# A two-layer graph network on one NeuronCore: the first part with an on-chip sort and a turned edge MLP in place of a dealt scatter

## The chip, the cores and the metric

The kernel runs on one NeuronCore of a Trainium2 chip. The metric is the device time of one execution in microseconds (us), the median over several executions; lower is better.

## The reference, cut to what matters

There are 3125 nodes with 128 features and 100000 edges, sorted by `dst`, with 64 features each. Two graph layers follow each other, each with a residual sum and a layer norm. The change lies in what comes before the first layer's softmax: the MLP on the edges (three small heads), and the records that both layers read.

```python
h = node_features @ node_fc_W + node_fc_b
he = edge_features @ edge_fc_W + edge_fc_b
t = relu(einsum('ed,mdf->emf', he, rel_att_W1) + rel_att_b1)      # m = 3, f = 128
g = sigmoid(einsum('emf,mf->em', t, rel_att_W2) + rel_att_b2)     # 3 numbers for each edge
a = sum(h[src] * h[dst]);  alpha = seg_softmax(a, dst);  beta = seg_softmax(g, dst)
h_att = segment_sum(alpha * (h[src] @ node_att_W), dst)
h_rel = segment_sum(beta * (h[src] @ rel_att_W), dst)
# layer 1: softmax over the edges of one src
e = tanh(q[src] + k[dst]);  alpha = exp(e @ Wphi) / segment_sum(..., src)
out = segment_sum(alpha * (vy[dst] + e @ We), src)
```

## The kernel before, in words

The program is a row of blocks, and all engines end one before the next begins.

**The first part** (lines 300 to 790) makes two tables of records in DRAM: `rec0`, the edges in `dst` order with src, dst and the three exponentials of the sigmoids (10 words), and `rec1`, the pairs (src, dst) grouped by blocks of 125 source nodes, which layer 1 reads. An edge table in SBUF has 125 lanes by 800 edges. VectorE (DVE) counts how many edges of each lane fall into each of 25 blocks (L622), for both keys. A plan is made of the counts: 220 steps for each layer, each a group of 512 edges with a block of nodes. Then DVE works out each edge's place in `rec1` (`place_step`, L661 to L667, four operations on 125x800 for each of 25 blocks), and GpSimd scatters the pairs, 125 at a time, by indirect DMA (`scatter`, L414, 580 of them); DVE stages them (L691, L696). The last 220 columns of the edge table (`late`) are scattered in the next block, one for each of its steps (L859).

The MLP runs in the same part, 200 chunks of 500 edges. SyncE (SP) loads a chunk; TensorE (PE) transposes it (L508), ScalarE (ACT) copies the result to SBUF (L586), PE multiplies four times with the folded weights (L517, 125 edges by 384 hidden values each, with the bias as an extra row), and DVE takes each of the 12 pieces of 125x128 through relu, product with W2 and sum in one operation (`weigh`, L703). Scatter staging, the places in `dst` order and `weigh` alternate in DVE's queue by a fixed order (`deal_turn`); `dealt` semaphores hold DVE until a slot's scatter has landed. Then come the sigmoid, the exponentials and a split of the weights into three bf16 parts (L758 to L762), and four DMAs store `rec0` (L368).

**The second block** (L840 to L1070) is layer 0, 220 steps of 512 edges. In each step SP loads a record group and a block of h, GpSimd issues one scatter of `late` (L859) and four gathers of 128 rows of h (L863) into a ring of five, PE transposes them (L879, L885), makes scores (L896) and sums (L909, L912, L918), ACT and DVE do the softmax and the accumulation (L1005, L1019). **The fourth block** is layer 1 with the same steps over `rec1` (L1361 gathers kv rows); the third and the last block are per-node work.

Of the kernel before, what the change touches and what calls it, by code (L numbers as in the profile page):

```python
# [24 lines left out]
M = 3  # L25
# [16 lines left out]
LATE = STEPS  # L42
EARLY = (EL - LATE) // 4
DEAL = 6
SLOTS1 = 3
# [7 lines left out]
PIECES = 4  # L53
assert EL % PIECES == 0
assert EARLY * 4 + LATE == EL and EARLY == DEAL * (NB - 1) + 1 and DEAL == 2 * SLOTS1
# [18 lines left out]
def build(nc, i, out):  # L74
    with ExitStack() as ctx:
# [15 lines left out]
        rec1 = dram("rec1", [PADDED, W2], I32)  # L91
        plan_d = [dram(f"plan_d{l}", [STEPS, 2], I32) for l in range(2)]
        rec0_v = rec0.rearrange("(g p j) w -> g p (j w)", p=128, j=GT)
        rec1_v = rec1.rearrange("(g p j) w -> g p (j w)", p=128, j=GT)
# [28 lines left out]

        late = sb("late", [LANES, LATE, 1 + W2], I32)

# [57 lines left out]
        with ExitStack() as c1:  # L183
# [7 lines left out]
            scratch = rel_st[:, :, :].rearrange("p b n -> p (b n)")  # L191

            def part(n, dt=F32):
                return scratch[0:LANES, n * EL:(n + 1) * EL].bitcast(dt)

            src_i, dst_i = part(0, I32), part(1, I32)
            blk, sel, run, place, zero = (part(n) for n in range(2, 7))
            place_i = [part(n, I32) for n in (7, 8)]
            sel2, run2 = part(9), part(10)
            pair = sb1("pair", [LANES, EL, 2], I32)  # L200
            cnt = sb1("cnt", [LANES, 2, NB])
            tot = sb1("tot", [128, 2, NB])
            incl = sb1("incl", [128, 2, NB])
            off = sb1("off", [128, 2, NB])
            first = sb1("first", [LANES, 2, NB])
# [4 lines left out]
            cmp_t = sb1("cmp_t", [GH, 2, 2, NB - 1])  # L210
# [9 lines left out]
            pad1 = sb1("pad1", [PAD_LANES, GT, W2], I32)  # L220
# [5 lines left out]
            weT = sb1("weT", [DE, DE + 1])  # L226
            w1 = sb1("w1", [DE, M, D])
            w1b = sb1("w1b", [1, M * D])
            w2 = sb1("w2", [LANES, M, D])
            b2 = sb1("b2", [LANES, M])  # L230
            last_row = sb1("last_row", [1, DE + 1])
            wc = sb1("wc", [128, M * D])
            whole = sb1("whole", [LANES, 1])
            flag = sb1("flag", [1, 1], I32)
            iota_e = sb1("iota_e", [LANES, EL])
# [5 lines left out]
            ea = sb1("ea", [LANES, U, 4 * DE])  # L241
            eaT = sb1("eaT", [128, 2, 4 * LANES])
            hid = sb1("hid", [LANES, 4, M, D])
            glog = sb1("glog", [LANES, U, 4 * M])
            eg = y_sb[:, :, :].rearrange("p b d -> p (b d)")[0:LANES, 0:EL * M]
            rem = att_st[:, :, :].rearrange("p b d -> p (b d)")[0:LANES, 0:EL * M]
            U16 = mybir.dt.uint16
            rec_all = arena[0:LANES, 0:EL * RW].bitcast(I32).rearrange("p (e w) -> p e w", w=RW)
            rec_f = arena[0:LANES, 0:EL * RW].rearrange("p (e w) -> p e w", w=RW)
            rec_b = arena[0:LANES, 0:EL * RW].bitcast(BF16).rearrange("p (e w) -> p e w", w=2 * RW)  # L250
            rec_h = arena[0:LANES, 0:EL * RW].bitcast(U16)
            st_rec0 = sb1("st_rec0", [LANES, U, 4 * RW], I32)
            st_rec1 = sb1("st_rec1", [LANES, U, 4 * W2], I32)
# [3 lines left out]
            edges_in = sem1("edges_in")  # L257
            weights_in = sem1("weights_in")
            counted = sem1("counted")
# [11 lines left out]
            staged = [sem1(f"staged{l}") for l in range(2)]  # L271
            dealt = [[sem1(f"dealt{l}_{k}") for k in range((U, SLOTS1)[l])] for l in range(2)]
# [3 lines left out]
            folded = sem1("folded")  # L276
            x_in = sem1("x_in")
# [11 lines left out]
            tiled = sem1("tiled")  # L289
            g_sb = sem1("g_sb")  # L290
            biased = sem1("biased")
            flag_ps = sem1("flag_ps")
            flagged0 = sem1("flagged0")
            flagged = sem1("flagged")
            in_order = sem1("in_order")
            linear = sem1("linear")
            sig = sem1("sig")
            weighed = sem1("weighed")

            ea_dram = i["edge_attr_64"].rearrange("(p t) c -> p (t c)", p=LANES)  # L300
            WEIGHT_DMAS = 21

            with nc.Block() as block:
                @block.sync
                def _(sp):
# [5 lines left out]
                        (we[:, :], i["L0_gnn_edge_fc_W"]), (weT[:, DE:], col(i["L0_gnn_edge_fc_b"])),  # L311
                        (w1[:, :, :], i["L0_gnn_rel_att_W1"].rearrange("m d f -> d m f")),
                        (w1b[:, :], row(i["L0_gnn_rel_att_b1"].rearrange("m f -> (m f)"))),
                        (w2[:, :, :].rearrange("p m f -> p (m f)"),
                         i["L0_gnn_rel_att_W2"].rearrange("m f -> (m f)").partition_broadcast(LANES)),
                        (b2[:, :], i["L0_gnn_rel_att_b2"].partition_broadcast(LANES)),
# [8 lines left out]
                        (w_e1[:, :], i["L1_gnn_We"]), (phi_b[:, :], i["L1_gnn_Wphi"].partition_broadcast(128)),  # L325
                        (x_sb[:, :, :], i["x"].rearrange("(b p) d -> p b d", p=BN)),
                    ]
                    assert len(loads) == WEIGHT_DMAS
# [3 lines left out]
                    sp.wait_ge(pads, 4)  # L332
                    sp.dma_start(rec0[E:, :].rearrange("(p j) w -> p (j w)", j=GT),
                                 pad0[:, :, :].rearrange("p j w -> p (j w)")).then_inc(pads_out, 16)
                    sp.dma_start(rec1[E:, :].rearrange("(p j) w -> p (j w)", j=GT),
                                 pad1[:, :, :].rearrange("p j w -> p (j w)")).then_inc(pads_out, 16)
# [8 lines left out]
                    for k in range(U):  # L345
                        sp.dma_start(ea[:, k, :], ea_dram[:, k * 4 * DE:(k + 1) * 4 * DE]).then_inc(ea_in[k], 16)

                    sp.wait_ge(plan_ready, 1)
                    for l in range(2):
                        sp.dma_start(plan_d[l].rearrange("(p h) k -> p (h k)", h=2),  # L350
                                     plan_i[0:STEPS // 2, l, :, :].rearrange("p h k -> p (h k)")).then_inc(plan_out, 16)
                    sp.wait_ge(plan_out, 32)
                    for l in range(2):
                        flat_plan = plan_d[l].rearrange("s k -> (s k)")
                        sp.dma_start(plan_row[l][:, :], row(flat_plan)).then_inc(plan_in, 16)
                        sp.dma_start(plan_b[:, l, :, :].rearrange("p s k -> p (s k)"), flat_plan.partition_broadcast(128)).then_inc(plan_in, 16)
                    with sp.Fori(1, CHUNKS // U) as c:
                        for k in range(U):
                            sp.wait_ge(ea_ps, U * c + k + 1 - U)
                            sp.dma_start(ea[:, k, :], ea_dram[:, bass.ds((c * U + k) * 4 * DE, 4 * DE)]).then_inc(ea_in[k], 16)  # L360

                    sp.wait_ge(flagged, 1)
                    ordered = sp.value_load(flag[0:1, 0:1], min_val=0, max_val=1)
                    with sp.If(ordered == 1):
                        for n in range(PIECES):
                            cols = slice(n * EL * RW // PIECES, (n + 1) * EL * RW // PIECES)
                            sp.wait_ge(in_order, n + 1)
# [167 lines left out]
                def _(act):  # L535
# [51 lines left out]
                    for k in range(U):  # L587
                        turned(0, k, k < 2)
# [1123 lines left out]
```

## Time and profile before

| what | us |
|---|---|
| median of 3 runs | 4611.61 (4606.64 to 4620.9) |
| the profiled execution | 4621.28, its span 4619.5 |
| busy PE, DVE, POOL, ACT | 3162.4, 2799.3, 2950.0, 1186.1 |
| mean granted TensorE clock | 0.815 of full |

Engines' busy times overlap, so they don't add up to the span. A time in the rows below is a place in the span; a group's "idle before" is how long its engine stood still ahead of it, with what released it.

### The profile page before, as it was taken

How to read it: one execution, taken by the hardware profiler on the slowest of the kernel's cores; microseconds unless marked ns; L12 is line 12 of the kernel's file. 1: busy time of each engine (PE TensorE's matmuls, PEld its weight loads, DVE VectorE, ACT ScalarE, POOL GpSimd, SP SyncE). 2: the span in 40 equal slices, each digit the busy share in tenths (PEclk: the TensorE clock that was granted, in tenths of full speed). 3: DMA queues.
4: the chain of work that ended last, by engine and by line, in shares of the span. 5: the costliest groups of instructions: out<-in, count | busy, mean ns of one | idle time of the engine just before them, and what ended most of it. 6: DMA issues, size and time to landing. Idle time of an engine off the chain costs nothing. (4 is left out here: it accounts for less than half of the span.)

```text
span 4619.5 us, 75532 instructions
## 1 busy us (share of the span) xinstructions
PE 3162.4 (68%) x16479; PEld 2217.2 (48%) x16479; DVE 2799.3 (61%) x11134; ACT 1186.1 (26%) x3211; POOL 2950.0 (64%) x2590
## 2 busy tenths in 40 slices
PE   5177777776477887878878777855666666666664
PEld 3043444443255555555555555634545554554453
DVE  5977777777455555555555555564555555555554
ACT  2011111111133333333333333412222222222222
POOL 0088888886467777777767777405666666666661
PEclk9599899898688998888889889955777677767776
DMA  2011111111211221211212212102222222222221
GB/s 70 4 29 29 29 28 29 28 28 22 68 42 44 45 45 43 45 43 43 45 41 45 44 44 45 24 23 67 69 71 71 71 71 71 71 70 70 71 70 28
DMA packets 298189, 218.99 MB, mean 47 GB/s; under 512 B 215607, under 2 KB 269234, under 8 KB 298144
## 3 DMA queue, kind: packets, MB, share of 16 engines
q0 software_dynamic: 96000, 146.02, 13.7%
q1 hardware_dynamic: 202144, 72.47, 6.8%
q8 instruction: 15, 0.25, 0.0%
q14 instruction: 30, 0.25, 0.0%
HBM read 203.84 MB, written 13.22 MB: 47 GB/s over the span
## 5 line engine op out<-in xcount | busy, mean ns | idle before, releaser
L1361 POOL DMA_INDIRECT arena<-kv_table,rec_sb x880 | 906.4, 1030 | 479.4 <-issue 238.8
L863 POOL DMA_INDIRECT arena<-h_table,rec x880 | 998.3, 1134 | 270.4 <-issue 262.5
L414 POOL DMA_INDIRECT rec<-st_rec,st_at x580 | 737.4, 1271 | 387.6 <-issue 386.4
L517 PE MATMUL bank<-wc,eaT 128*125 128x384 f32 x1600 | 626.5, 539 | 327.1 <-DVE hid L703 221.9
L909 PE MATMUL bank<-arena 128*128 128x375 f32 x1760 | 617.5, 494 | 0.0
L1407 PE MATMUL bank<-arena,probT 128*125 128x193 f32 x1760 | 513.5, 456 | 118.0 <-DVE probT L1525 61.7
L517 PEld LDWEIGHTS bank<-wc,eaT 128*125 128x125 f32 x1600 | 295.3, 204 | 566.4 <-DVE hid L703 260.7
L703 DVE SCALAR_TENSOR_TENSOR hid<-bank,w 125x128 f32<-125x128 f32 x2400 | 525.9, 285 | 11.3 <-PE bank L517 8.7
L1407 PEld LDWEIGHTS bank<-arena,probT 128*125 128x125 f32 x1760 | 423.2, 266 | 175.1 <-DVE probT L1525 99.2
L909 PEld LDWEIGHTS bank<-arena 128*128 128x128 f32 x1760 | 355.8, 202 | 314.0 <-issue 137.8
L1005 DVE CUSTOM_DVE_ANT_0 score<-bank,mask,m_old 125x512 f32<-125x512 f32 x220 | 165.1, 750 | 463.1 <-remote 269.5
L859 POOL DMA_INDIRECT rec<-late_at x220 | 297.2, 1351 | 201.9 <-remote 103.2
L990 DVE TENSOR_TENSOR arena<-onehot,rec 128x1500 f32<-128x1500 bf16 x220 | 377.1, 1714 | 0.0
L1401 PE MATMUL bank<-top_run,ones 1*128 1x1 f32 x440 | 106.7, 309 | 369.4 <-issue 168.2
L586 ACT COPY eaT<-bank 64x500 f32<-64x500 f32 x200 | 113.8, 569 | 912.1 <-PE bank L508 863.3
L901 PE MATMUL bank<-identf,prob 125*128 125x125 f32 x880 | 152.0, 300 | 283.0 <-ACT prob L952 160.9
L1401 PEld LDWEIGHTS bank<-top_run,ones 1*128 1x128 f32 x440 | 88.0, 248 | 454.1 <-issue 235.0
L896 PE MATMUL bank<-hsT,hbT 128*125 128x512 f32 x440 | 288.0, 742 | 0.0
L1451 ACT COPY hotT<-bank 125x512 bf16<-125x512 bf16 x220 | 128.1, 582 | 588.6 <-remote 539.7
L948 ACT COPY probT<-bank 128x500 f32<-128x500 f32 x220 | 126.8, 576 | 522.8 <-PE bank L901 299.7
L918 PE MATMUL bank<-arena,probT 128*125 128x129 f32 x1760 | 249.9, 284 | 14.5 <-ACT probT L948 8.3
L901 PEld LDWEIGHTS bank<-identf,prob 125*128 125x128 f32 x880 | 110.3, 154 | 297.7 <-ACT prob L952 167.8
(261 smaller groups left out, 5246.0 us busy)
## 6 DMA issues: line engine op xcount, KB each, us to landing
ea<-in_edge_attr SPq DMA_DIRECT2D x200, 125.0 KB
arena<-h_table,rec POOLq DMA_INDIRECT x880
arena<-kv_table,rec_sb POOLq DMA_INDIRECT x880
hbT<-hT_table SPq DMA_DIRECT2D x220, 62.5 KB
qb<-q_table SPq DMA_DIRECT2D x220, 46.9 KB
rec<-st_rec,st_at POOLq DMA_INDIRECT x580
rec<-rec SPq DMA_DIRECT2D x220, 20.0 KB
rec<-arena SPq DMA_DIRECT2D x4, 976.6 KB
```

The source lines that it names most:

```text
L414: pool.indirect_dma_start(out=table, out_offset=bass.IndirectOffsetOnAxis(ap=st_at[:, k, j:j + 1], axis=0), in_=ring[:, k, j * words:(j + ...
L517: pe.matmul(bank[1 + j][0:LANES, 0:M * D], eaT[:, k % 2, j * LANES:(j + 1) * LANES], wc[:, :], start=True, stop=True).then_inc(hid_ps, 1)
L703: last = v.scalar_tensor_tensor(hid[:, j, m, :], bank[1 + j][0:LANES, m * D:(m + 1) * D], 0.0, w2[:, m, :], ALU.max, ALU.mult, accum_out=g ...
L859: pool.indirect_dma_start(out=rec1, out_offset=bass.IndirectOffsetOnAxis(ap=late_at[:, k, 0:1], axis=0), in_=late_at[:, k, 1:], in_offset= ...
L863: pool.indirect_dma_start(out=hs[:, k % RING, j, 0:D], out_offset=None, in_=h_table, in_offset=bass.IndirectOffsetOnAxis(ap=rec_v[:, k, j, ...
L896: pe.matmul(bank[2][0:BN, :], hbT[:, k, :], hsT[:, k % 2, :], start=True, stop=True).then_inc(score_ps, 1)
L901: last = pe.transpose(bank[3][:, j * BN:(j + 1) * BN], prob[:, k % 2, j * 128:(j + 1) * 128], identf[0:BN, 0:BN])
L909: pe.matmul(bank[6 + k % 2][:, 0:M * BN], hs[:, k % RING, j, 0:D], hot_w_v[:, k % 2, j, :], start=(j == 0), stop=(j == GT - 1))
L918: last = pe.matmul(bank[4 + k % 2][0:BN, 0:D + 1], probT_v[:, k % 2, j, :], hs[:, k % RING, j, :], start=(j == 0), stop=(j == GT - 1))
L990: v.tensor_tensor(hot_w[:, k % 2, :].rearrange("p (j m n) -> p j m n", j=GT, m=M), onehot_v[:, k % RING, :, :].unsqueeze(2).to_broadcast([ ...
L1361: pool.indirect_dma_start(out=row_v[:, k % RING, j, 0:KV], out_offset=None, in_=kv_table, in_offset=bass.IndirectOffsetOnAxis(ap=rec_v[:, ...
L1407: last = pe.matmul(bank[4 + k % 2][0:BN, 0:KV + 1], probT_v[:, k % 2, j, :], row_v[:, k % RING, j, AD:RK], start=(j == 0), stop=(j == GT - 1))
```

## The change

The first part is rewritten; the second block loses its scatter; the fourth reads `rec1` in another layout. The rest is as before.

1. **Sort in SBUF.** Keys `src * 4096 + dst`, exact in f32, fill a tile of 128x1024, padded. A bitonic network sorts them: phases 1 to 10 lie within a partition, 55 exchanges; for phases 11 to 17 PE transposes the tile (`turn_keys`, 8 transposes of 128x128 at 15 places), DVE takes the result out of PSUM and does 98 further exchanges. An exchange is a minimum and a maximum of 128x512. Counts are made for `dst` alone. The sorted keys are decoded into `pair1` and stored by one DMA. The `rec1` scatters, the staging, the places in `dst` order and `late` are gone.
2. **Turned MLP.** 100 octets of 1000 edges. PE transposes four 125x128 pieces; six matmuls for each octet have 64 rows of contraction (upper or lower half of the partitions by turns) and 500 columns and give hidden values on partitions, edges on columns, in four PSUM banks by turns. ACT evicts them with bias and relu. For each pair of octets 12 matmuls with a shifted 128x32 weight collect the logits of 20 octets in one bank, each in its own 32 of the partitions. After 20 octets logits are transposed back, and tanh and exp follow (`gates`), then `split` and a store: five times instead of once at the end.
3. **DVE's share.** From octet 66 on DVE takes two of the six evictions.

```diff
+            TURN_AT = [5 + 7 * (n // 2) + 3 * (n % 2) for n in range(15)]
+            TOTS_AT, REACH_AT = 2, 60
+            SHARED = 66
+            SPLIT_AT = {68 + 4 * n: n for n in range(3)} | {86: 3}
+            act_share = lambda o: 2 * M if o < SHARED else 2 * M - 2
...
-                            pe.matmul(bank[1 + j][0:LANES, 0:M * D], eaT[:, k % 2, j * LANES:(j + 1) * LANES], wc[:, :],
-                                      start=True, stop=True).then_inc(hid_ps, 1)
+                    def hidden(o):
+                        pe.wait_ge(ea_sb, o + 1)
+                        for n in range(2 * M):
+                            m, half = n // 2, n % 2
...
+                            pe.matmul(bank[1 + (6 * o + n) % 4][:, 0:4 * LANES], wc[half * DE:(half + 1) * DE, m * D:(m + 1) * D],
+                                      eaT[half * DE:(half + 1) * DE, o % 3, :], start=True, stop=True).then_inc(hid_ps, 1)
+                    def logits(o):
...
+                        for m in range(M):
+                            for j in range(4):
+                                at = 31 - (M * q + m)
+                                last = pe.matmul(bank[5][32 * j:32 * j + 32, 0:4 * LANES], w2_shift[:, m, at:at + 32],
+                                                 hid[(o - 1 + j // 2) % 3 * 6 + 2 * m + j % 2],
+                                                 start=(q == 0 and m == 0), stop=(q == TILE // 2 - 1 and m == M - 1))
...
+                    for o in range(OCTS):
+                        if o + 2 < OCTS:
+                            turn(o + 2)
+                        if o + 1 < OCTS:
+                            hidden(o + 1)
+                        if o >= TILE and o % TILE == 0:
+                            turn_logits(o // TILE - 1)
+                        if o % 2:
+                            logits(o)
+                        if o in TURN_AT:
+                            turn_keys(TURN_AT.index(o))
...
+                    def rectified(o):                                      # ACT
...
+                        for n in range(act_share(o)):
+                            m = n // 2
+                            act.wait_ge(hid_ps, 6 * o + n + 1)
+                            act.activation(hid[o % 3 * 6 + n], bank[1 + (6 * o + n) % 4][:, 0:4 * LANES], ACT.Relu,
+                                           bias=bias1[:, m:m + 1]).then_inc(hid_sb, 1)
...
+                    def exchange(lo, hi, out_lo, out_hi, after):           # DVE
+                        v.wait_ge(sorted_, after)
+                        v.tensor_tensor(out_lo, lo, hi, ALU.min).then_inc(sorted_, 1)
+                        v.tensor_tensor(out_hi, lo, hi, ALU.max).then_inc(sorted_, 1)
...
+                    for o in range(SHARED, OCTS):
+                        rectified(o)                                       # DVE: tensor_scalar, add and max, n = 4 and 5
+                        if o in SPLIT_AT:
+                            split(SPLIT_AT[o])
...
-                            pool.indirect_dma_start(
-                                out=rec1, out_offset=bass.IndirectOffsetOnAxis(ap=late_at[:, k, 0:1], axis=0),
-                                in_=late_at[:, k, 1:], in_offset=None).then_inc(gathered[k % RING], 16)
...
-                            sp.dma_start(rec[:, k, :], rec1_v[bass.ds(g, 1), :, :].rearrange("o p w -> (o p) w")).then_inc(loaded[k], 16)
+                            sp.dma_start(rec[:, k, :], rec1[:, bass.ds(g, 1), :].rearrange("p o w -> p (o w)")).then_inc(loaded[k], 16)
```

## Rows read from the trace of the kernel before

**Rows 1.** Windows: busy us of each engine, granted clock, DMA share, GB/s
```profile
0.00:100.00 100.00, 54.62 (x157) 33.58 (x158) 55.44 (x130) 27.76 (x152) 6.22 (x26) 1.00 0.26 71
205.00:1142.00 937.00, 696.30 (x2380) 381.98 (x2380) 697.76 (x5406) 113.41 (x198) 737.41 (x580) 0.91 0.17 28
1142.00:1205.00 63.00, 0.20 (x3) 0.12 (x3) 33.27 (x37) 6.30 (x6) 6.41 (x7) 0.50 0.20 72
1205.00:2976.00 1771.00, 1405.47 (x7480) 997.92 (x7480) 978.24 (x2418) 581.16 (x1100) 1289.27 (x1094) 0.89 0.20 43
3150.00:4619.00 1469.00, 897.12 (x5986) 727.40 (x5985) 834.84 (x2728) 406.73 (x1587) 899.97 (x874) 0.71 0.26 67
```

**Rows 2.** Groups by line and form, 205 to 1142 us: busy, mean ns, idle before
```profile
L414 POOL DMA_INDIRECT rec<-st_rec,st_at x580 | 737.4, 1271 | 387.6 <-issue 386.4 <-DVE st_rec L696 1.2
L703 DVE SCALAR_TENSOR_TENSOR hid<-bank,w 125x128 f32<-125x128 f32 x2400 | 525.9, 285 | 11.3 <-PE bank L517 8.7 <-issue 0.5
L703 DVE DVE_READ_ACCUMULATOR hid<-bank,w 125x1 f32 x2400 | 197.3, 82 | 0.7 <-issue 0.6
L691 DVE COPY st_at<-rel_st 125x4 int32 x138 | 25.1, 182 | 218.1 <-DMA rec<-st_rec,st_at 215.2 <-issue 2.6
```

**Rows 3.** Timeline around TensorE's start on the edges: start, us
```profile
93.10 0.44 PE L461 MATMUL bank<-identf,hblk 125*128 125x125 f32 x1 [0.47 <-ACT hT L561]
99.30 2.03 PE L480 MATMUL bank<-reach_diag,ones 98*128 98x98 f32 x8 [4.32 <-DVEq L649]
108.32 1.01 PE L508 MATMUL bank<-identf,ea 125*64 125x125 f32 x4 [0.77 <-ACT w_fold L580]
```

**Rows 4.** Timeline of two chunks of the MLP on TensorE
```profile
1132.82 0.59 PE L508 MATMUL bank<-identf,ea 125*64 125x125 f32 x4
1133.24 2.75 PE L517 MATMUL bank<-wc,eaT 128*125 128x384 f32 x8
```

**Rows 5.** Timeline of VectorE in the first part
```profile
9.82 0.58 DVE L606 COPY pair<-rel_st 125x800 int32<-125x800 int32 x1 [9.69 <-DMA rel_st<-in_dst]
14.40 0.98 DVE L622 TENSOR_SCALAR_CACHE_REDUCE rel_st<-rel_st 125x800 f32<-125x800 f32 x1
15.31 0.98 DVE L622 TENSOR_SCALAR_CACHE_REDUCE rel_st<-rel_st 125x800 f32<-125x800 f32 x1
196.85 1.87 DVE L665 TENSOR_TENSOR rel_st<-rel_st 125x800 f32<-125x800 f32 x2
1154.20 0.78 DVE L759 TENSOR_TENSOR att_st<-arena 125x600 f32<-125x600 f32 x1
1155.02 0.61 DVE L760 CAST arena<-att_st 125x600 bf16<-125x600 f32 x1
```

**Rows 6.** Timeline of the end of the first part and the start of layer 0
```profile
1141.91 2.66 DVE L737 TENSOR_TENSOR y_sb<-y_sb,b 125x2400 f32<-125x2400 f32 x1
1146.82 1.28 ACT L598 ACT_TABLE_LOAD   x1
1168.44 0.26 SPq L368 DMA_DIRECT2D rec<-arena  x1
1190.80 0.14 POOL L852 MEMSET arena<- 128x20 f32 x1 [57.49 <-POOLq L303]
1204.99 1.09 PE L879 MATMUL bank<-identf,arena 128*128 128x128 f32 x4 [56.88 <-DMA arena<-h_table,rec]
```

**Rows 7.** Groups by line and form, 1205 to 2976 us
```profile
L863 POOL DMA_INDIRECT arena<-h_table,rec x876 | 994.5, 1135 | 269.2 <-issue 261.2 <-PE bank L918 7.6 <-remote 0.3
L859 POOL DMA_INDIRECT rec<-late_at x218 | 294.8, 1352 | 195.6 <-remote 103.2 <-issue 49.5 <-PE bank L918 42.8
L948 ACT COPY probT<-bank 128x500 f32<-128x500 f32 x220 | 126.8, 576 | 522.8 <-PE bank L901 299.7 <-remote 197.9 <-issue 15.4
L1022 DVE TENSOR_TENSOR rel_st<-rel_st,bank 128x375 f32 x220 | 118.4, 538 | 0.2 <-issue 0.2
```

**Rows 8.** Timeline of layer 0: the first sum of consecutive steps on VectorE
```profile
2016.84 0.35 DVE L1019 SCALAR_TENSOR_TENSOR att_st<-att_st,shrink,bank 125x129 f32 x1
2022.54 0.35 DVE L1019 SCALAR_TENSOR_TENSOR att_st<-att_st,shrink,bank 125x129 f32 x1 [0.70 <-PE bank L918]
2029.34 0.35 DVE L1019 SCALAR_TENSOR_TENSOR att_st<-att_st,shrink,bank 125x129 f32 x1 [1.75 <-PE bank L918]
```

More of the change, by code:

```diff
@@ L352, in _ @@
[L352 to L360, printed above, removed]
@@ L520, in edge_body @@
-                    def edge_body(c, first=False, final=False):
-                        for k in range(U):
-                            if not (final and k == U - 1):
-                                turn(c + (k + 1) // U, (k + 1) % U)
-                            hidden(c, k, first and k == 0)
-                    turn(0, 0, True)
-                    edge_body(0, True)
-                    with pe.Fori(1, CHUNKS // U - 1) as c:
-                        edge_body(c)
-                    edge_body(CHUNKS // U - 1, final=True)
@@ L577, in _ @@
                     act.wait_ge(folded_ps, 3)
-                    act.copy(wc[0:DE + 1, :], bank[0][0:DE + 1, 0:M * D]).then_inc(folded, 1)
+                    for m in range(M):
+                        act.activation(bias1[:, m:m + 1], bank[3][:, m:m + 1], ACT.Identity, bias=b1[:, m:m + 1]).then_inc(folded, 1)
+                    act.copy(bias2[:, :], bank[3][:, M:M + 1]).then_inc(folded, 1)
                     act.wait_ge(folded_ps, 4)
+                    act.copy(wc[:, :], bank[0][:, 0:M * D]).then_inc(folded, 1)
@@ new lines, in _ @@
+                    turned(0)
+                    turned(1)
+                    rectified(0)
+                    for o in range(OCTS):
+                        if o + 2 < OCTS:
+                            turned(o + 2)
+                        if o >= TILE and o % TILE == 0:
+                            keep_logits(o // TILE - 1)
+                        if o + 1 < OCTS:
+                            rectified(o + 1)
+                        if o >= TILE and o % TILE == 0:
+                            gates(o // TILE - 1)
@@ L671, in _ @@
-                    v.sem_inc(deal, 1)
-                    step(v.memset(place, 0.0))
-                    with v.Fori(0, NB // 2) as b:
-                        for part in range(4):
-                            for side in range(2):
-                                behind = max(2 * part + side - 1, 0) if part < 3 else 5 + 2 * side
-                                v.wait_ge(deal, b * 8 + 1 + behind)
-                                place_step(1, 2 * b + side, part, (sel, sel2)[side], (run, run2)[side])
```

675 lines of the change are left out of this document (398 added, 277 removed).

## The prediction

> **What bounds the kernel now.** I read the windows by stage first [rows 1]: 4619.5 us of span fall into a first part up to 1205, layer 0 from 1205 to 2976, some 174 us of per-node work, and layer 1 from 3150. The change touches the first two and one small load of the last. Then the groups of the edge MLP [rows 2]: between 205 and 1142 us DVE is fed `weigh` in 2400 pieces, 525.9 + 197.3 = 723 us (697.8 as a union), and it stands 215 us ahead of L691 for a scatter to land. GpSimd's 580 scatters take 737 busy and 388 of gaps. So the first part is held by DVE and by the scatter in turn, and TensorE, at 696 of 937 us, waits for them. The chunk's rows show TensorE's own pace [rows 4]. In layer 0 the groups of GpSimd are what to see [rows 7]: 994.5 + 294.8 busy and 269.2 + 195.6 idle is the stage, of which only about 154 us (103.2 + 42.8 + 7.6, the waits for "remote" and L918) are real waiting. In each of the 220 steps it needs 7.4 of 8.0 us.
>
> **The MLP, turned.** Removed: all 200 chunks with `weigh`, and with them DVE's 723 us. Added for each octet of 1000 edges: 4 transposes, 6 hidden matmuls and 6 logit matmuls (12 for a pair). An f32 matmul is recorded as two passes (eight L517 for four matmuls), and eight passes of 384 columns take 2.75 us, of which some 0.2 is the last one's tail: 0.32 us a pass, so 0.415 for 500 columns [rows 4]. Transposes: 0.6 us for four [rows 4].
> If passes run strictly one after another, an octet is 24 x 0.415 + 0.6 = 10.6 us. That is the upper end at full clock. The lower end is what evicts: ACT has six relus and one copy of 500 columns at 0.576 [rows 7], 4.0 us, up to octet 65, and five, 2.9, from 66.
> No row has two matmuls in separate parts of the array, as this change issues them: hidden matmuls alternate between rows 0-63 and 64-127, logit matmuls between four groups of 32 columns. [...] Six hidden matmuls are then 7 pass times, twelve logit matmuls 13: (7 + 6.5) x 0.415 + 0.6 = 6.2 us an octet. It lies between the ends, nearer to ACT's 4.0 (where the engine after it would be full) than to 10.6.
> [...]
> 100 octets: 620 us. The biases ride in the evictions, at nothing.
>
> **When it starts and ends.** TensorE finishes h at 93.5 us and begins the edges at 108.3, with 4.3 of wait and 2.0 of work for the plan between [rows 3]; both move behind octet 60, four small bias matmuls come in: start at 104. It meets the counts after `logits` of octet 1, near 118. DVE has them at: start 9.8, keys 1.5, 55 exchanges, 10 sign changes at some 0.6, then 1 + 1 + 2.5 for the flag and block numbers and 25 counts at 0.91 [rows 5]. An exchange: two independent operations of 800 columns take 1.87 us [rows 5]; 0.98 for one of 800 and 0.78 for one of 600 give 1.0 ns a column, so 1.27 for two of 512, and 0.04 for the wait between chained ones (1154.20 + 0.78 to 1155.02) makes 1.31. Sum: 9.8 + 1.5 + 72 + 6 + 4.5 + 22.7 = 117. TensorE doesn't wait for more than a few us. The strides of near exchanges cost nothing: L759 reads a strided tile at that rate.
> Later phases: between two turns DVE has at most 7 exchanges, or 10 and a copy, 9 to 16 us with the eviction and the turn; TensorE comes by after 3 or 4 octets, 18.6 or 24.8 us. So the 98 exchanges, 128 us, lie beside the MLP and cost nothing; below 4 us an octet they would begin to hold TensorE, which is queued in order behind each turn. Their 15 x 8 transposes are TensorE's own: 1.2 us a turn, 18. The counts of `src` (22.7 us), the places (50 rounds of four operations) and the staging leave DVE too; they are not counted apart, since the stage is replaced as a whole.
> Ends of tiles: four times ACT loads two tables (1.28 each [rows 6]), a tanh and eight small exps, some 5 us, of which I take 2.5 as seen: 10.
> Tail: now 1142 to 1205 [rows 6]: bias, sigmoid, exp, split 27 us; last store issued 1168.4, next block 1190.8, first transpose 1205. With four fifths of it done earlier: 10 for the last logits, gates and split, 8 for one store of a fifth, 14 for the block's start: 32.
> First part: 104 + 620 + 18 + 10 + 32 = 784 against 1205: **421 less**.
>
> **DVE's share.** From octet 66 two evictions of 500 columns from PSUM (0.538 for 375 [rows 7], so about 0.67) go to DVE, 1.3 us of an octet of 6.2; ACT falls from 4.0 to 2.9. Beside TensorE at 6.2 both are covered: 0. If TensorE needs only 4.9, ACT's 4.0 plus bank waits come near, and it is worth 0 to 0.5 us x 34, at most 17. What is behind the new wait is `split`, wanted only at a store ten octets later.
>
> **Layer 0 without the scatter.** GpSimd loses 1.352 + 0.897 (195.6 / 218) us a step; 4 x (1.135 + 0.298) = 5.7 stay [rows 7]. TensorE has 1405.5 / 220 = 6.4 busy [rows 1]. Neighbouring undisturbed steps are 5.7 and 6.8 us apart [rows 8]. The mean now is 1771 / 220 = 8.05. Ends: 0 if the scatter is beside another wait that stays, 220 x (8.05 - 5.7) = 517 if only the fast steps remain. I take 6.7, TensorE's 6.4 and some waiting: 220 x 1.35 = **297 less**. SP's third load (`late_at`) goes too; SP isn't late.
>
> **Layer 1.** The same gathers, but a group's kv rows come in the order of (src, dst), so scattered, where before they were nearly ascending. Layer 0's h rows are scattered already, and the DMA engines are busy for a fifth of that stage and a quarter of this [rows 1]. I take 0; the bounds are 30 less and 60 more.
>
> **Sum.** 4621.3 (the profiled execution, 1.8 outside its span) - 421 - 297 = 3903; the median of the runs shown is 9.7 below the profiled one: **3894**.
>
> **Rivals.**
> *More overlap (four column groups at once).* The four logit matmuls of a head run together. From the pass time of [rows 4]: 12 logit matmuls in 3 x 2 passes, an octet (7 + 3) x 0.415 + 0.6 = 4.8, above ACT's 4.0, 4.9 with bank waits: 130 less, **3764**. [...]
> *Passes one after another, layer 0 gains.* 10.6 us an octet: 440 more than my 620, **4334**. For it: no row shows an overlap.
> *Overlap, but layer 0 stays.* The slow steps of layer 0 are not the scatter's: GpSimd was at 1289 of 1771 busy and does wait. 3894 + 297 = **4191**.
> *Slower: TensorE binds both places.* Passes one after another at the granted clock of that stretch, 0.91 [rows 1]: 9.96 / 0.91 + 0.6 = 11.5 an octet, a first part of 104 + 1155 + 60 = 1319, 114 more; and in layer 0 TensorE's order, not GpSimd, sets 8.05, so nothing comes back: 4612 + 114 = **4726**. It decides from 10.4 us an octet, where the first part alone is as long as now. Against: DVE's 723 us and the landing waits are certainly gone, and TensorE was idle for a fifth of layer 0.
>
> **How the numbers follow.** Forecast 0.46, more overlap 0.23, serial with a gain in layer 0 0.16, layer 0 unchanged 0.09, slower 0.06. Own range of the likeliest: 3740 to 4060 (an octet of 5.7 to 6.8, layer 0 at 6.2 to 7.3 us). The range of 3680 to 4360 takes in the three next cases and leaves out the slower one and the ends of the others. 0.3% is what a measurement of this kernel tells from no change: faster 0.93, same 0.01, slower 0.06.
>
> **What would show it.** The timeline of the hidden matmuls: an octet's six within 3.0 us show the overlap, 5.0 refute it; a pair's twelve logit matmuls in 5.4 (mine), 2.6 (more overlap) or 10. First transpose of layer 0 near 784. ACT's relus waiting for TensorE, not the other way. TensorE's waits at the turns near zero, else the sort holds it. Steps of layer 0 at 6.7 us with GpSimd near 5.7 of them. I am wrong if an octet is over 7.5 us, or if layer 0 keeps 8 us a step.

## The result, and the profile after

| | us | ratio to the kernel before, same chip |
|---|---|---|
| before, median of 4 | 4609.12 (4604.09 to 4620.9) | |
| changed, median of 4 | 3867.49 (3834.35 to 3869.38) | 0.8361 (0.8314 to 0.8408) |
| predicted | 3894 (3680 to 4360) | |

The changed kernel is 742 us faster, and the forecast is 27 us above the measured median. The profiled execution took 3834.35, the fastest of its four, so its stages add up to some 33 us under that median; the profiled execution of the kernel before was the slowest of its four, 12 us above the median, so the -787 of the profiles is 45 more than the median's -742. Stages by the profile, cut at the starts of the first transpose of layer 0, the last attention matmul of layer 0, and the first and last attention matmul of layer 1:

| kernel | first part | layer 0 | between | layer 1 | last block | span |
|---|---|---|---|---|---|---|
| before | 1205.0 | 1770.3 | 196.0 | 1366.1 | 82.1 | 4619.5 |
| changed | 694.7 | 1499.7 | 191.7 | 1365.9 | 80.6 | 3832.6 |
| difference | -510.3 | -270.6 | -4.3 | -0.2 | -1.5 | -786.9 |
| predicted | -421 | -297 | | 0 | | -718 |

The windows by stage, as in [rows 1]: two stretches of the MLP, the second with DVE's share; layer 0; layer 1.

```profile
99.00:382.00 283.00, 279.89 (x1476) 114.96 (x1475) 137.62 (x240) 204.15 (x365) 0.00 (x0) 1.00 0.16 49
470.00:640.00 170.00, 168.86 (x881) 63.34 (x881) 52.38 (x80) 94.52 (x167) 0.00 (x0) 1.00 0.20 66
683.00:2270.00 1587.00, 1378.13 (x7705) 993.38 (x7705) 1044.44 (x2574) 601.19 (x1178) 981.50 (x880) 0.93 0.20 48
2390.00:3832.00 1442.00, 902.15 (x5954) 731.62 (x5954) 830.76 (x2709) 403.11 (x1577) 887.03 (x860) 0.70 0.26 68
```

Where TensorE was at 696 of 937 us, waiting for `weigh` and the scatter, it is now busy 99% of the MLP at a granted clock of 1.00. It is the bound of the first part; DVE, with the sort on it, is at 49%, ACT at 72% and, with DVE's share, at 56%.

The MLP on TensorE (start, us, number of passes): one pair of octets, where [rows 4] have a chunk. From one pair's first transposes to the next pair's, 638.27 to 649.14, are 10.87 us, 5.4 for an octet.

```profile
638.27 0.65 PE L531 MATMUL bank<-identf,ea 125*128 125x125 f32 x4
638.85 3.60 PE L545 MATMUL bank<-eaT,wc 64*128 64x500 f32 x12
642.38 0.65 PE L531 MATMUL bank<-identf,ea 125*128 125x125 f32 x4
642.96 3.60 PE L545 MATMUL bank<-eaT,wc 64*128 64x500 f32 x12
646.49 2.29 PE L558 MATMUL bank<-arena,w_shift 128*32 128x500 f32 x18
649.14 0.65 PE L531 MATMUL bank<-identf,ea 125*128 125x125 f32 x4
```

The pair's logits are 24 passes (a pass is one record of an f32 matmul, which has two); the row of 646.49 holds the first 18, the other six follow between 648.20 and 649.2.

The groups of 130 to 450 us (busy, mean ns, idle before): TensorE's weight loads for the hidden matmuls stand 59.6 us for a relu to empty a bank. The two operations of an exchange last 699 and 690 ns and overlap a little; exchanges in a row start 1.33 us apart (18.42 and 19.75, for two undisturbed ones).

```profile
L678 ACT ACTIVATE arena<-bank,bias 128x500 f32<-128x500 f32 x298 | 175.3, 682 | 19.9 <-PE bank L545 17.5
L545 PEld LDWEIGHTS bank<-eaT,wc 64*128 64x128 f32 x672 | 73.9, 185 | 91.6 <-ACT arena L678 59.6 <-issue 30.1
L725 DVE TENSOR_TENSOR keys<-rel_st 128x512 f32<-128x512 f32 x46 | 32.2, 699 | 1.6
L726 DVE TENSOR_TENSOR keys<-rel_st 128x512 f32<-128x512 f32 x46 | 31.7, 690 | 0.0
```

The timeline where TensorE meets the counts: they are ready at 117.6, TensorE comes by at 122.05 without a wait, and DVE is the one that stood.

```profile
118.52 3.60 PE L545 MATMUL bank<-eaT,wc 64*128 64x500 f32 x12
122.05 0.40 PE L595 MATMUL bank<-cnt,ltri 125*125 125x25 f32 x2
122.94 0.15 DVE L783 TENSOR_SCALAR flag<-bank 1x1 int32<-1x1 f32 x1 [5.34 <-PE bank L597]
```

The start of the edges and the end of the first part, beside [rows 3] and [rows 6]:

```profile
99.96 1.07 PE L531 MATMUL bank<-identf,ea 125*128 125x125 f32 x4 [0.77 <-ACT w_fold L657]
667.46 0.68 ACT L670 ACTIVATE logit<-bank,bias 128x500 f32<-128x500 f32 x1 [3.87 <-PE bank L558]
674.14 0.28 SPq L383 DMA_DIRECT2D rec<-rel_st  x1
682.33 0.13 POOL L1001 MEMSET arena<- 128x20 f32 x1 [648.26 <-POOLq L333]
694.78 1.09 PE L1024 MATMUL bank<-identf,arena 128*128 128x128 f32 x4 [25.82 <-DMA arena<-h_table,rec]
```

Layer 0's gathers and layer 1's, by group, where [rows 7] have the first:

```profile
L1008 POOL DMA_INDIRECT arena<-h_table,rec x880 | 981.5, 1115 | 512.8 <-issue 244.9
L1506 POOL DMA_INDIRECT arena<-kv_table,rec_sb x880 | 906.8, 1030 | 475.0 <-issue 239.3
```

```text
span 3832.6 us, 66795 instructions
## 1 busy us (share of the span) xinstructions
PE 2973.6 (78%) x17025; PEld 2031.4 (53%) x17025; DVE 2242.8 (59%) x6015; ACT 1438.7 (38%) x3691; POOL 1902.1 (50%) x1791
## 5 line engine op out<-in xcount | busy, mean ns | idle before, releaser
L1008 POOL DMA_INDIRECT arena<-h_table,rec x880 | 981.5, 1115 | 512.8 <-issue 244.9
L1506 POOL DMA_INDIRECT arena<-kv_table,rec_sb x880 | 906.8, 1030 | 475.0 <-issue 239.3
L1054 PE MATMUL bank<-arena 128*128 128x375 f32 x1760 | 608.3, 488 | 0.0
L1552 PEld LDWEIGHTS bank<-arena,probT 128*125 128x125 f32 x1760 | 424.9, 267 | 164.2 <-DVE probT L1670 102.9
L545 PE MATMUL bank<-eaT,wc 64*128 64x500 f32 x1200 | 360.8, 616 | 0.3 <-ACT arena L678 0.3
L678 ACT ACTIVATE arena<-bank,bias 128x500 f32<-128x500 f32 x488 | 288.0, 681 | 43.8 <-PE bank L545 41.1
L1097 ACT ACTIVATE prob<-score,m_neg 125x512 f32<-125x512 f32 x220 | 158.8, 722 | 338.8 <-DVE m_neg L1153 299.7
L1041 PE MATMUL bank<-hsT,hbT 128*125 128x512 f32 x440 | 269.6, 698 | 0.0
L1046 PE MATMUL bank<-identf,prob 125*128 125x125 f32 x880 | 143.3, 288 | 148.3 <-ACT prob L1097 75.9
L1063 PE MATMUL bank<-arena,probT 128*125 128x129 f32 x1760 | 248.6, 283 | 0.0
L545 PEld LDWEIGHTS bank<-eaT,wc 64*128 64x128 f32 x1200 | 131.2, 186 | 166.2 <-ACT arena L678 106.1
L1641 DVE TENSOR_TENSOR arena<-bank,arena 128x256 f32<-128x256 f32 x220 | 92.7, 421 | 209.9 <-remote 196.8
L1063 PEld LDWEIGHTS bank<-arena,probT 128*125 128x125 f32 x1760 | 212.1, 187 | 0.0
```

Source lines behind the costliest of these rows:

```text
L545: pe.matmul(bank[1 + (6 * o + n) % 4][:, 0:4 * LANES], wc[half * DE:(half + 1) * DE, m * D:(m + 1) * D], eaT[half * DE:(half + 1) * DE, o ...
L678: act.activation(hid[o % 3 * 6 + n], bank[1 + (6 * o + n) % 4][:, 0:4 * LANES], ACT.Relu, bias=bias1[:, m:m + 1]).then_inc(hid_sb, 1)
L1008: pool.indirect_dma_start(out=hs[:, k % RING, j, 0:D], out_offset=None, in_=h_table, in_offset=bass.IndirectOffsetOnAxis(ap=rec_v[:, k, j, ...
L1041: pe.matmul(bank[2][0:BN, :], hbT[:, k, :], hsT[:, k % 2, :], start=True, stop=True).then_inc(score_ps, 1)
L1054: pe.matmul(bank[6 + k % 2][:, 0:M * BN], hs[:, k % RING, j, 0:D], hot_w_v[:, k % 2, j, :], start=(j == 0), stop=(j == GT - 1))
L1063: last = pe.matmul(bank[4 + k % 2][0:BN, 0:D + 1], probT_v[:, k % 2, j, :], hs[:, k % RING, j, :], start=(j == 0), stop=(j == GT - 1))
```

## The experiments

Three groups ran, each on a chip of its own. The changed kernel was run again in the first (median 3848.07, ratio 0.8343, 0.8326 to 0.8359) and the third (3894.26, 0.8348, 0.8327 to 0.8369). The first part is 694.4 to 695.1 us in the three profiles of it, wherever it ran; layers 0 and 1 are mostly some 15 to 30 us longer on the other two chips (layer 1: 1365 to 1373 in the first group, 1385 to 1391 in the others), so they are compared within a group. Within one they spread too: layer 0, which nothing of the first group edits, is 1500, 1507, 1512 and 1526 us there. The second group's four kernels ran once each, so their times are read by the stages of their profiles.

> The changed kernel itself, as the yardstick for the three beside it. Both theories: 3867 us within 0.3%, 742 below the kernel before.

> The changed kernel once more, as the yardstick for the two beside it: 3850 to 3867 us, first part 694.5 us up to layer 0's first transpose.

Both medians missed what was expected, the first by 0.5% below 3867, the second by 0.7% above it, and the kernel before moved with them (4617 and 4667); the ratios agree.

**How much do tiled matmuls overlap? Logits, column group by column group.** The 12 matmuls of a pair in another order, so that neighbours use the same 32 columns of the array.

```diff
-                        for m in range(M):
-                            for j in range(4):
+                        for j in range(4):
+                            for m in range(M):
```

> The twelve logit matmuls of a pair of octets in another order: three in a row for each group of 32 columns, instead of four groups by turns. Theory 1 (neighbours in separate column groups run at once, neighbours in one group one after another): the 24 passes go from 2.7 us to about 9 (3 x 4 x 2 x 0.415 = 10 less overlaps at the three changes of group), 50 times 6.3 = 315 us more. Rival (the array spreads any twelve of them, or reorders them): no change.

Measured (one execution): 4020.89, first part 823.8, so 129 us more, between the 315 of the theory and the 0 of the rival. The timeline of a pair, from its logits' first pass to the next transposes:

```profile
564.45 3.63 PE L558 MATMUL bank<-arena,w_shift 128*32 128x500 f32 x18
569.69 0.65 PE L531 MATMUL bank<-identf,ea 125*128 125x125 f32 x4
```

5.24 us instead of 2.65: 50 x 2.6 = 130, the whole difference. In the changed kernel the logits' passes start four at a time, 0.42 apart (646.49, 646.93, 647.35, 647.77), so a head's four matmuls run together through both of their passes. Even grouped by column they don't fall back to one after another, which would be 24 x 0.42 = 10. I read four chains of six passes in the starts, 0.42 apart in each, which begin at 564.45, 565.32, 566.19 and 567.06: a group starts when the one before it is at its third pass, so two groups, and at times three, run beside each other. By this reading a group's first matmul starts 0.83 us before the third of the group ahead of it (565.32 against 566.15), which stands earlier in the program.

**Hidden matmuls, first the three of the lower rows, then the three of the upper** (the evictions' biases and the logits' inputs follow).

```diff
-                            m, half = n // 2, n % 2
+                            m, half = n % M, n // M
```

> The six hidden matmuls of an octet in another order: three on rows 0-63, then three on rows 64-127, instead of by turns. Theory 1 (an upper and a lower one overlap): 3.54 us becomes 11 x 0.415 + 0.6 = 5.2, 1.6 us an octet, 160 us more. Rival (the six are paced by the evictions, and overlap is worth nothing there): less than 40 us more.

Measured (one execution): 3936.82, first part 729.4, 35 us more: the number is the rival's, and the theory's 160 is refuted, but not because overlap is worth nothing, as the starts show. An octet's hidden passes, 3.87 us instead of 3.60 (27 of the 35 us), and ACT's third relu:

```profile
561.54 3.87 PE L545 MATMUL bank<-eaT,wc 64*128 64x500 f32 x12
564.35 1.24 ACT L678 ACTIVATE arena<-bank,bias 128x500 f32<-128x500 f32 x2 [0.16 <-PE bank L545]
```

Its passes start at 561.54, 562.06, 562.48, 562.49, 562.90, 563.01, 563.32, 563.47, 563.74, 563.99, 564.41 and 564.83. I read two chains in them: the lower rows' six passes from 561.54 to 563.74, and the upper rows' six from 562.49 to 564.83. Then the fourth matmul of the program (the first on the upper rows) starts at 562.49, before the third's first pass, at 563.32. By that reading the fourth matmul, on the upper rows, didn't wait for the third, which was queued for the busy lower ones and started 0.83 us later. The rows don't name the half, so the assignment is my reading; that two passes overlap fully is plain from starts 0.01 us apart. ACT bears the reading out: its third relu waits for TensorE until 564.35, just behind the end of the pass of 563.74 (0.58 long). Were the third matmul the one of the passes at 562.49 and 563.01, the relu could have gone on at 564.19, when the second one ended. The logits grouped by column show the same sign (565.32 against 566.15).

**What holds the hidden matmuls to 3.60?** Twelve passes two by two are 6 x 0.415 and a tail, 2.7. In the changed kernel they start at 638.85, 639.37, 639.79, 640.21 in twos; the fifth matmul starts at 640.78, when a relu has emptied the first of the four banks, and the sixth at 641.35, when the next relu has emptied the second:

```profile
640.78 0.29 PEld L545 LDWEIGHTS bank<-eaT,wc 64*128 64x128 f32 x2 [0.79 <-ACT arena L678]
641.35 0.29 PEld L545 LDWEIGHTS bank<-eaT,wc 64*128 64x128 f32 x2 [0.27 <-ACT arena L678]
```

Four kernels change the order around these waits.

DVE takes the second and fourth eviction of an octet instead of the last two (TensorE's waits and ACT's list follow):

```diff
+            TAKEN = (1, 3)
-                        for n in range(act_share(o), 2 * M):
+                        for n in TAKEN:
```

> From octet 66 on DVE takes the second and fourth eviction instead of the fifth and sixth, so that two engines empty the first banks side by side. Theory 1 (the fifth and sixth hidden matmul wait for the first and second relu): only the sixth one's wait goes, at most 0.3 us an octet in 34 octets, 0 to 10 us less. Rival (TensorE's own passes): no change.

Measured (median of 5): 3841.68, ratio 0.8312 (0.8294 to 0.8329), which overlaps the changed kernel's own interval; first part 681.3, so 13.1 less than the 694.4 of its group, a little above the 0 to 10 of the theory. Hidden matmuls from octet 66:

```profile
621.25 3.15 PE L547 MATMUL bank<-eaT,wc 64*128 64x500 f32 x12
623.17 0.41 PEld L547 LDWEIGHTS bank<-eaT,wc 64*128 64x128 f32 x4 [0.79 <-ACT arena L680]
```

0.45 x 34 octets = 15 us, about what the stage shows. The first bank comes back no sooner: the fifth matmul starts 1.92 us after the first here (623.17) and 1.93 in the changed kernel (640.78), with the same wait of 0.79. What goes is the sixth one's own wait, as the theory had it: DVE empties the second bank beside ACT's first, and the weights of both matmuls are loaded in one row, where they stood 0.57 us apart. Where ACT empties the first two banks one after the other (the changed kernel, with or without DVE's share), that wait stays.

The next octet's transposes between the fourth and fifth hidden matmul:

```diff
                     for o in range(OCTS):
+                        if o + 1 < OCTS:
+                            hidden(o + 1, range(4))
                         if o + 2 < OCTS:
                             turn(o + 2)
                         if o + 1 < OCTS:
-                            hidden(o + 1)
+                            hidden(o + 1, range(4, 2 * M))
```

> TensorE does the transposes of octet o+2 between the fourth and the fifth hidden matmul of octet o+1 instead of before the first, and ACT copies them after its second relu. Theory 1 (the fifth hidden matmul waits about 0.4 us for the first relu to free its bank, and nothing stands in that gap): the transposes fill it, 0.4 us an octet, 40 us less in all. Rival (six hidden matmuls take 3.5 us by TensorE's own passes): no change, or some us more, since ACT's relus now stand behind the copy.

Measured (median of 5): 3834.2, ratio 0.8306 (0.8286 to 0.8326); first part 678.1, 16.3 less of the 40 that the theory had. The rival is refuted, and the wait has moved rather than gone: the fifth and sixth matmul (562.10) follow the transposes at once, but the next octet's first (563.50) now waits for the third relu, which ACT does behind its copy (timeline, and the wait in brackets):

```profile
562.10 1.15 PE L545 MATMUL bank<-eaT,wc 64*128 64x500 f32 x4
562.20 0.57 ACT L666 COPY eaT<-bank 128x500 f32<-128x500 f32 x1
562.67 1.25 ACT L680 ACTIVATE arena<-bank,bias 128x500 f32<-128x500 f32 x2
563.47 0.29 PEld L545 LDWEIGHTS bank<-eaT,wc 64*128 64x128 f32 x2 [1.04 <-ACT eaT L666]
563.50 2.00 PE L545 MATMUL bank<-eaT,wc 64*128 64x500 f32 x7 [0.26 <-ACT arena L680]
```

The pair's logits between the fourth and fifth hidden matmul of every other octet, and the transposes there in the rest:

```diff
-                        if o + 2 < OCTS:
+                        if o % 2 and o + 2 < OCTS:
                             turn(o + 2)
                         if o + 1 < OCTS:
-                            hidden(o + 1)
+                            hidden(o + 1, range(4))
+                        if o % 2:
+                            logits(o)
+                        elif o + 2 < OCTS:
+                            turn(o + 2)
+                        if o + 1 < OCTS:
+                            hidden(o + 1, range(4, 2 * M))
```

> The wait ahead of the fifth hidden matmul is filled in every octet: with the logit matmuls where the octet has them, with the transposes of the octet after next where it has none (ACT copies those after its second relu). Theory (that wait is what is left to gain beside the passes): a pair of octets goes from 10.87 us to 9.1 us, ACT's 14 evictions of 0.585 being 8.2; the first part 60 to 85 us shorter, near 620. Rival (ACT's own work, 8.2 us a pair in a fixed order, comes to bind, as where the transposes alone were put inside and only 16 of 40 us came): 10.3 us a pair, 25 us shorter.

Measured (median of 5): 3882.93, ratio 0.8327 (0.8302 to 0.8351), which overlaps the changed kernel's; first part 683.0, 12.1 less than the 695.1 of its group. That is neither the theory's 60 to 85 nor the rival's 25, and less than the transposes alone gave. Twelve hidden passes in a row are still there once a pair, behind the logits, the last two matmuls of one octet and the first four of the next, and they still wait:

```profile
561.17 3.75 PE L545 MATMUL bank<-eaT,wc 64*128 64x500 f32 x12
563.18 0.29 PEld L545 LDWEIGHTS bank<-eaT,wc 64*128 64x128 f32 x2 [0.87 <-DVE arena L882]
```

And with DVE's alternate share on top:

> The same, and from octet 66 on DVE takes the second and fourth eviction instead of the fifth and sixth. Theory: 5 to 15 us below the one before it, since ACT has then 5.8 us of evictions a pair. Rival (the waits are all filled already): no difference.

Measured (median of 5): 3877.0, ratio 0.8307 (0.8288 to 0.8327); first part 674.0, 21.1 less, and 9 below the kernel before it, as its theory had. It is the fastest first part of all and 17 us below the changed kernel of its group by the medians; the intervals just touch (0.8327 and 0.8327), so by the times alone the gain is probable, and by the stage it is plain.

**DVE's share alone.** ACT keeps all six evictions to the end.

```diff
-            act_share = lambda o: 2 * M if o < SHARED else 2 * M - 2
+            act_share = lambda o: 2 * M
```

> ACT keeps all six evictions up to the last octet. Theory 1 (TensorE binds, the share is hidden): no change, within 5 us of the changed kernel. Rival (ACT's evictions bind, six at 0.585 against four): the 34 octets after the 66th get longer by up to 1.2 us each, 40 us more, 1.0%.

Measured (median of 6): 3860.56, ratio 0.8342 (0.8314 to 0.837) against 0.8343; first part 695.0 against 694.4. The share is worth nothing: the median is 12 us above the changed kernel's 3848.07, but the two sets of times overlap (3830 to 3875 and 3837 to 3861), and the stage is the same. Layer 0 was 1525.5 in this one profile, 13 to 26 more than in the three others of its group, though nothing of it was edited; it stays unexplained. This execution took 3861.95, so the changed kernel's own spread between 3834 and 3869 may lie in layer 0; no profile of a slower execution of the changed kernel on that chip tells.

**Layer 0: what was the scatter's?** A scatter of one pair of integers for each of 125 lanes, to unused memory, ahead of each step's gathers, in their queue and with their semaphore (the third load of SP doesn't come back):

```diff
+                            pool.indirect_dma_start(
+                                out=dump, out_offset=bass.IndirectOffsetOnAxis(ap=dump_at[0:LANES, k:k + 1], axis=0),
+                                in_=rec[0:LANES, k, 0:W2], in_offset=None).then_inc(gathered[k % RING], 16)
-                        pe.wait_ge(gathered[k % RING], 64 * turn_of(s, k))
+                        pe.wait_ge(gathered[k % RING], 80 * turn_of(s, k))
```

> The changed kernel with one scatter of 125 pairs (8 bytes each, into an unused table) put back ahead of the four gathers in each of layer 0's 220 steps. The source is the step's own record, so SP's third load does not come back. Theory 1 (GpSimd's queue binds layer 0, and the scatter was worth the 265 us by which the stage got shorter): layer 0 back to some 1750 us from 1506, the whole near 4100. Rival (the stage got shorter by something else, the third load or the clock): under 80 us more.

And in its place a GpSimd memset of the same length, without a transfer:

```diff
+                            pool.wait_ge(cleared, s * SU + k + 1)
+                            pool.sem_inc(ticks, 1)
+                            pool.memset(y_sb[:, 0:12, :], 0.0).then_inc(cleared, 1)
```

> The changed kernel with a memset of 125x1536 on GpSimd, about 1.3 us, ahead of the four gathers in each of layer 0's 220 steps, and no DMA. Theory 1 (it is the scatter's time on GpSimd, 1.35 us, that counts, whatever it moves): layer 0 longer by nearly as much as with the scatter, 150 to 260 us. Rival (it is the transfer of 8-byte pairs in the queue of the gathers): under 60 us more.

Measured (one execution each): 4127.68 with the scatter, layer 0 1760.7; 3940.38 with the memset, layer 0 1582.0. Layer 0 unedited was 1530.2 and 1538.8 in the two other kernels of this group, 1534.5 in the mean: the scatter costs 226 us, as its theory had (some 1750), and the memset 47, which is its rival's number (under 60). With the spread of 26 us that the unedited stage has in the first group, 226 is safe and 47 is rough. The groups on GpSimd of layer 0, with the scatter:

```profile
L1015 POOL DMA_INDIRECT arena<-h_table,rec x876 | 1008.6, 1151 | 269.7 <-issue 263.0 <-PE bank L1070 4.9 <-remote 1.8
L1011 POOL DMA_INDIRECT dump<-rec,dump_at x218 | 296.0, 1358 | 170.0 <-remote 87.8 <-issue 52.3 <-PE bank L1070 30.0
```

with the memset:

```profile
L1011 POOL DMA_INDIRECT arena<-h_table,rec x876 | 1026.5, 1172 | 235.6 <-issue 199.3 <-POOL y_sb L1009 34.9 <-PE bank L1066 1.4
L1009 POOL MEMSET y_sb<- 125x1536 f32 x218 | 304.4, 1396 | 0.1
```

and the two unedited stages (logits by group, hidden by half), whose gathers have most of their idle time in real waits:

```profile
L1008 POOL DMA_INDIRECT arena<-h_table,rec x875 | 971.9, 1111 | 541.9 <-issue 238.9 <-PE bank L1063 167.4 <-remote 135.5
L1008 POOL DMA_INDIRECT arena<-h_table,rec x875 | 970.1, 1109 | 551.7 <-issue 240.9 <-PE bank L1063 176.6 <-remote 134.2
```

Read as an account of GpSimd's stage: unedited it has 971 of work, 240 of issue gaps and 307 of waits in the mean. The memset adds 360 of work (304 and longer gathers) and takes 271 of the waits and 41 of the gaps: it moved into time in which GpSimd stood anyway, until GpSimd itself was full (1331 + 199 of 1567), and the stage grew only by what didn't fit. The scatter adds 334 of work and 75 of issue gaps, and takes only 183 of the waits; 124 of waits remain, 88 of them for "remote" just ahead of the scatter. So beside much the same GpSimd time, a scatter has 116 us more of issue gaps and 88 more of waits than the memset. Whether those 88 are its landing, which TensorE waits for here as in the kernel before, or its place ahead of the gathers in the queue, was not told apart.

This account leaves out TensorE's clock, and that moved as well. Layer 0 in the windows of [rows 1], with the scatter, with the memset, and unedited (logits by group):

```profile
696.90:2457.90 1761.00, 1403.16 (x7480) 995.26 (x7480) 983.46 (x2418) 582.02 (x1100) 1304.65 (x1094) 0.89 0.19 43
696.20:2278.50 1582.30, 1312.88 (x7480) 916.73 (x7480) 1009.79 (x2418) 584.27 (x1100) 1329.94 (x1094) 0.99 0.20 48
823.80:2354.30 1530.50, 1351.97 (x7480) 966.50 (x7480) 975.97 (x2418) 575.55 (x1100) 971.56 (x875) 0.94 0.20 50
```

The granted clock is 0.89 with the scatter, as in the kernel before, 0.94 unedited and 0.99 with the memset, and TensorE's same 7480 passes are busy 51 us longer with the scatter and 39 shorter with the memset. So up to some 50 of the scatter's 226 us may be slower work on TensorE, and the memset's 47 may hide up to some 40 that a clock of 0.94 would have shown. Whether the clock is a cause here, or only follows from where TensorE stands still, no run tells apart.

## Why the prediction was right

**Which engine, where: right.** DVE's 723 us and the landing waits went, and TensorE took over as the bound of the first part, at a granted clock of 1.00.

**An octet, 6.2 us: 5.4 measured, the step that failed.** The 7 and 13 pass times, one more than there are matmuls, were an estimate of mine, and no run shows them. The runs showed both passes of neighbouring matmuls in separate parts of the array run together: four logit matmuls start within 0.02 us and their second passes 0.44 us later, again within 0.02 (646.49 and 646.93), hidden ones two by two within 0.01 (638.85, and 639.37 for the second passes). The term "logit matmuls 13" pass times was mis-sized: a pair's logits take 2.65 us to the next transposes, as the rival *more overlap* had it (2.6), against my 5.4. Grouping them by column cost 129 us, two or three at a time instead of four. "Six hidden matmuls are then 7 pass times" came out near, 3.53 us to the next transposes against 2.9, but for another reason: two by two they would be about 2.7 with the tail, and the waits for the first and second relu fill them up to 3.6; where DVE takes alternate banks the second wait goes and they are 3.15. So the sign "ACT's relus waiting for TensorE, not the other way" did not hold for the fifth and sixth matmul. Of the two errors the logits gave 1.35 us an octet back and the bank waits took 0.6: 0.75 x 100, most of the 89 us by which the first part was shorter than forecast. The rival's 4.9 us an octet is nearer to the 5.4 measured than my 6.2, and its first part (654) is nearer to the 694.7 than my 784; what it lacked is most of the bank waits.

Four column groups of 32 give nearly the factor four here: 24 passes in 2.65 us against 24 x 0.415 = 10.0. A change from one kind of matmul to the next shows in two places: the first start after it is 0.51 us behind the last one of the old kind instead of 0.42 (645.98 to 646.49, 648.63 to 649.14), and the hidden matmuls' second start 0.52 behind their first (638.85, 639.37, 639.79). The 0.52 also stands where they only waited (640.78 to 641.30), so a change costs at most some 0.2 us, and no run without changes prices it. At 0.2 us each, the five changes in a pair of octets are at most 0.5 us of an octet's 5.4, by my estimate.

**Start, turns, sort, tail: right.** Start 99.96 (104), counts ready at 117.6 (117), an exchange 1.33 us (1.31), turns 15 x about 1.0 (18), from the last logits to layer 0's first transpose 27.3 (32). Start, turns and tail came out 3 to 5 us short each, which together with the octets' 75 makes up nearly all of the 89. The sort's 98 later exchanges cost nothing: TensorE never stood for them (of its 10.9 us of idle time ahead of the turns the profile puts none down to DVE). What the tail was cut from, a store of a fifth and a fifth of the gates, shows as the 6.7 us from 667.46 to 674.14. The 10 us for the ends of tiles counted two table loads of 1.28 us each; the profile has none between 99 and 700 us. At the first end the tanh is at 225.95 (0.63 us) and the eight exps follow at 226.61 (1.30 us).

**DVE's share, 0 (at most 17): right**, 0.6 by the profile of the kernel without it, and nothing that the times can tell. What the upper bound meant exists, and isn't reached by this share but by another: alternate evictions gave 13 us.

**Layer 0, -297: -271.** Steps came out at 6.74 us (6.7). The forecast was 26 too far because the stage holds 24 us besides the 219 distances between steps (1499.7 - 219 x 6.74), which I had spread over the steps of before (8.05) and left out of those of after; it is also no more than the 26 us by which the unedited stage varied. That the scatter is the cause is shown: put back alone, on another chip, it costs 226, and the stage had lost 271. The rest, some 45 us, may be SP's third load, the addresses or the chip; it was not tried. The mechanism that the prediction gave, GpSimd's own time, is the smaller part: 1.352 + 0.897 us a step went and the stage gave back 1.23, and the same time without a transfer costs 0.2 a step (at most 0.4 with the clock allowed for). The larger part is the issue gap and the waits that come with a DMA, and perhaps the clock. The 6.7 itself was in part luck: "TensorE's 6.4 and some waiting" became 6.1 (1348 / 220, at a clock of 0.94) and 0.6.

**Layer 1, 0 (-30 to +60): right**, 1366.1 and 1365.9, its gathers at 1030 ns in both, although the rows of a group are now scattered over the table.

**The median.** 3894 against 3867: by stages I was 89 too high in the first part, 26 too low in layer 0 and 6 too high in the rest, so 69 too high for the profiled execution (3903 against 3834). The forecast then went 10 down from profile to median, while the changed kernel's median lies 33 above its profile, within its own spread (3834 to 3869); no step of mine had that. 69 - 10 - 33 leaves the 27. The closeness is partly that luck.

## What to carry to other kernels

In these runs small f32 matmuls on separate rows or columns of the array cost as if they ran together, both passes of each (24 logit passes took 2.65 us by turns, 5.24 with neighbours on the same columns): order them so that neighbours use different parts, and count passes by the busiest part. Then count the banks: with four banks, the fifth hidden matmul waited 0.79 us for the first eviction and the sixth 0.27 for the second. Dividing the evictions between two engines helped only where it emptied the bank that was wanted next sooner; here that was the second (13.1 us less in the first part, against 0.6 for the last two evictions). The work taken off GpSimd gave back its time and its issue gap, less the waits that it had covered (put back as a memset, 304 us of it made layer 0 only 47 longer); look at how much of the stage's idle time is real waiting before pricing it. And compare the granted clock of a stage (0.89, 0.94 and 0.99 in layer 0 here) before laying a difference to one engine.

## What the runs showed of the hardware that I had not expected

- Four 128x32 f32 matmuls with 500 columns in four column groups start their passes within 0.02 us of each other and take 0.42 us a pass together; two groups, at times three, if issued by group (5.24 us for 24 passes).
- Of six 64-row matmuls issued three and three by half, the fourth seems to have started 0.8 us before the third; ACT's wait for the third agrees.
- TensorE kept the granted clock of 1.00 through 540 us of such matmuls and transposes in turn (99 to 640 us).
- In layer 0 the granted clock was 0.89 with a scatter in each step, 0.94 without, and 0.99 with a memset on GpSimd in its place.
- In one DMA queue, a scatter of 125 pieces of 8 bytes ahead of four gathers cost 226 us in 220 steps, 1.0 us each, where the same time of GpSimd without a transfer cost 0.2 (at the higher clock, 0.99 against 0.89).
